# Rows of 32 experts carried by indirect DMA instead of one-hot matmuls, with neighbouring experts interleaved

## What is computed

```
B, S, D = 2, 256, 256 (512 tokens);  E, G, K = 32, 8, 4;  hidden H = 512;  CAP_FACTOR = 1.25
scores of groups and experts -> the 4 best groups, in these the 4 best experts of each token
gate = softmax over the chosen experts
slot = how many earlier tokens chose the same expert; only slots below 80 = 512/32*4*1.25 are kept
out  = x + shared_expert(xn) + sum over kept choices of gate * expert_e(xn)
expert_e(v) = (silu(v @ wg[e]) * (v @ wu[e])) @ wd[e]          # 256 -> 512 -> 256, f32
```

## Time and profile before

| what | us |
|---|---|
| three runs | 2159.97, 2161.23, 2163.57; median 2161.23 |
| the profiled execution | 2161.95, with a span of 2160.1 from first to last instruction |
| PE busy | 1865.0 (86% of the span) |
| DVE, ACT, POOL busy | 1178.5, 865.4, 178.5 |
| mean granted PE clock | 0.918 of full speed |
| router block (first load issued to the last product of the shared expert) | 1031.7 to 1069.4 |
| experts (first pass of up to the sum with the residual) | 1072.65 to 1367.42 |

### The profile page before, as it was taken

The page is one execution under the profiler, slowest core; times in us unless marked ns, Lnnn a source line. Parts: engine busy times, 40 slices in busy tenths (PEclk is TensorE's granted clock), DMA queues, the critical chain, the costliest instruction groups (busy, mean ns, idle before and its releaser), DMA issues. The chain is left out here.

```text
span 2160.1 us, 38703 instructions
## 1 busy us (share of the span) xinstructions
PE 1865.0 (86%) x12958; PEld 1076.0 (50%) x12958; DVE 1178.5 (55%) x2155; ACT 865.4 (40%) x1654; POOL 178.5 (8%) x335
## 2 busy tenths in 40 slices
PE   8999799999999446588799999599999999383598
PEld 4444334444444224357599999344444444152476
DVE  5777588888886455364300000388887885372400
ACT  2222156666667123134211111166666666021121
POOL 2222200000000000010000000000000000000000
PEclk9999889999999768799799999699999999686699
DMA  5586654433340530000396665334343340502242
GB/s 187 185 223 192 161 86 62 59 58 58 58 58 16 135 42 1 0 1 17 114 262 225 226 196 171 48 45 60 58 58 58 58 62 12 82 8 80 78 136 68
DMA packets 148041, 200.20 MB, mean 93 GB/s; under 512 B 24712, under 2 KB 121744, under 8 KB 141608
## 3 DMA queue, kind: packets, MB, share of 16 engines
q1 hardware_dynamic: 145900, 197.34, 40.2%
q10 hardware_dynamic: 2064, 1.87, 0.3%
HBM read 160.25 MB, written 38.94 MB: 92 GB/s over the span
## 5 line engine op out<-in xcount | busy, mean ns | idle before, releaser
L1079 ACT ACTIVATE probs<-ps 128x512 f32<-128x512 f32 x1024 | 573.8, 596 | 287.7 <-PE ps L1006 276.3
L1091 DVE TENSOR_REDUCE top<-ps 128x1 f32<-128x1024 f32 x512 | 601.0, 1219 | 35.8 <-PE ps L987 33.4
L987 PE MATMUL ps<-kst,qst 105*128 105x512 bf16 x1024 | 318.7, 394 | 35.8 <-POOL qst L945 27.8
L1006 PE MATMUL ps<-qst,kst 105*128 105x256 bf16 x2048 | 344.6, 276 | 2.3 <-DVE qst L1103 1.8
L1020 PE MATMUL ps_o<-probs,vst 128*32 128x256 f32 x4096 | 328.6, 393 | 0.8 <-ACT probs L1079 0.8
L1006 PEld LDWEIGHTS ps<-qst,kst 105*128 105x128 bf16 x2048 | 176.3, 100 | 215.0 <-ACT probs L1079 66.1
L987 PEld LDWEIGHTS ps<-kst,qst 105*128 105x128 bf16 x1024 | 65.9, 98 | 189.8 <-DVE top L1091 90.5
L2035 DVE TENSOR_TENSOR hT<-silu,ps_h 128x320 f32<-128x320 f32 x32 | 15.6, 488 | 263.0 <-ACT silu L1996 263.0
L1020 PEld LDWEIGHTS ps_o<-probs,vst 128*32 128x32 f32 x4096 | 80.8, 108 | 109.9 <-issue 89.8
L477 PE MATMUL ps_k<-ctxT,wk 128*128 128x512 f32 x256 | 121.8, 599 | 2.1 <-DVE square_weights L642 2.1
L1959 PEld LDWEIGHTS ps_h<-xe,wgu 128*128 128x128 f32 x1024 | 119.3, 192 | 3.0 <-ACT xe L1985 0.2
(11 more groups left out here) (305 smaller groups left out, 2257.6 us busy)
## 6 DMA issues: line engine op xcount, KB each, us to landing
kst<-kd SPq DMA_DIRECT2D x384, 128.0 KB
kd<-kp SPq DMA_DIRECT2D x64, 384.0 KB, 2.6
wgu<-in_L_ffn_wg_dram SPq DMA_DIRECT2D x32, 512.0 KB, 3.8
wgu<-in_L_ffn_wu_dram SPq DMA_DIRECT2D x32, 512.0 KB, 4.6
wd<-in_L_ffn_wd_dram SPq DMA_DIRECT2D x32, 512.0 KB, 3.9
w<-in_L_ffn_w_dram SPq DMA_DIRECT2D x16, 1024.0 KB, 5.4
ctx_sb<-in_ctx_dram SPq DMA_DIRECT2D x16, 512.0 KB, 5.8
vd<-square_weights SPq DMA_DIRECT2D x16, 512.0 KB, 4.1
```

Of the source, the lines that this page charges most:

```text
L987: mm = pe.matmul(ps1[:, u % 2, x * 512:(x + 1) * 512], qst[:, m, qt * P:(qt + 1) * P], kst[:, m, c * W1 + x * 512:c * W1 + (x + 1) * 512], ...
L1006: mm = pe.matmul(ps2[:, u % 2, x, :], kst[:, m, kt * P:(kt + 1) * P], qst[:, m, :], start=True, stop=True)
L1079: nc.scalar.activation(probs[:, u % SLOTS, :, :], ps2[:, u % 2, :, :], ACT.Exp).then_inc(probs_ready, 1)
L1091: v.tensor_reduce(top[:, b, u // NC1, u % NC1:u % NC1 + 1], ps1[:, u % 2, :], AX, ALU.max).then_inc(mx, 1)
```

## The change

- route0 and the block of the experts become one block. There are no one-hot matrices any more: disp, comb, combT, gather, combine and the transposes of comb are gone, on PE, DVE, POOL and ACT.
- DVE makes, beside the gate, for each token the four row numbers (expert * 80 + slot) of its kept choices (row) and their shares (share). A choice that isn't kept gets a number out of bounds.
- A DRAM tensor expert_rows_in (2560 rows of 1 KB) is filled with zeros by SP, and then POOL scatters the rows of xn into it by 16 indirect DMAs (4 tiles x 4 choices, 128 rows each).
- For each expert SP loads its 80 rows (xr), PE turns them by two transposes (turn), ACT copies them to xe. After down, ACT copies ye, and SP stores it to expert_rows_out in DRAM.
- At the end POOL gathers the rows back by 16 indirect DMAs (back), and DVE adds them with 16 multiply-adds (128x256), after shared expert and residual have been put into dst earlier.
- PE's order for one expert is: turn(e+2), up(e+1), down(e). ps_h has two buffers (4 banks); ps_y lies in acc.
- SP's order for one expert is: rows of e+2 (xr), wgu of e+2, then, after ye of expert e is copied, wd of e+2, the store of ye.
- The loads for the next cross attention (kst, vall) are all issued ahead of the first xr; those of qall come in the following block (pieces_to_dram, before=), and qall is allocated only there.

The core of the diff (names that only move are left out):

```diff
-def route0(pr, st, xn, xT, acc, ahead):
+def experts0(pr, xn, xT, residual, dst, next_cross):
...
             @block.sync
...
-                ahead(sp)
+                sp.wait_ge(zero_set, 1)
+                sp.dma_start(xed.rearrange("(p r) d -> p r d", p=P), bc(zeros[:, :], 1, NROWS // P)).then_inc(zeroed, 16)
+                for e in range(2):
+                    load_gu(e)
+                    load_d(e)
+                for m in range(NBUF):
+                    next_cross.load_constant_rows(sp, m)
+                    next_cross.load_k(sp, m // B, m)
+                for part in range(VPARTS):
+                    next_cross.load_v(sp, part)
+                sp.wait_ge(scattered, 16 * NT * TOPK)
+                for e in range(2):
+                    load_x(e)
+                for e in range(E0):
+                    if e + 2 < E0:
+                        sp.wait_ge(x_turned, e + 1)
+                        load_x(e + 2)
+                        sp.wait_ge(h_made, e + 1)
+                        load_gu(e + 2)
+                    sp.wait_ge(y_copied, e + 1)
+                    if e + 2 < E0:
+                        load_d(e + 2)
+                    sp.dma_start(yed[e * CAP0:(e + 1) * CAP0, :], ye[:, e % 2, :]).then_inc(y_out[e % 2], 16)
+
+            @block.gpsimd
+            def _(pool):
+                nc.gpsimd.memset(zeros[:, :], 0.0).then_inc(zero_set, 1)
+                pool.wait_ge(zeroed, 16)
+                pool.wait_ge(row_ready, 1)
                 for t in range(NT):
+                    for k in range(TOPK):
+                        nc.gpsimd.indirect_dma_start(
+                            xed, bass.IndirectOffsetOnAxis(row[:, t, k:k + 1], 0), xn[:, t, :], None,
+                            bounds_check=NROWS - 1, oob_is_err=False).then_inc(scattered, 16)
+                pool.wait_ge(sh_added, 1)
+                nc.gpsimd.memset(back[:, :, :, :], 0.0).then_inc(zero_set, 1)
+                pool.wait_ge(zero_set, 2)
+                for b in range(2):
+                    pool.wait_ge(y_out[b], 16 * E0 // 2)
+                for t in range(NT):
+                    for k in range(TOPK):
+                        nc.gpsimd.indirect_dma_start(
+                            back[:, t, k, :], None, yed, bass.IndirectOffsetOnAxis(row[:, t, k:k + 1], 0),
+                            bounds_check=NROWS - 1, oob_is_err=False).then_inc(came_back[t], 16)
...
+                def turn(e, b, first=False):
+                    pe.wait_ge(x_in[b], 8 * (e - b) + 16)
+                    if not first:
+                        pe.wait_ge(x_copied, e - 1)
+                    for c in range(C):
+                        mm = pe.transpose(xview[:, b, c, :], xr[:, b, c * P:(c + 1) * P], pr.cf("ident")[0:CAP0, 0:CAP0])
+                    mm.then_inc(x_turned, 1)
...
                 def expert(e, b, place):
...
+                    if not place.startswith("last"):
+                        turn(e + 2, b)
+                    if place != "last":
+                        up(e + 1, 1 - b, first=(place == "first"))
+                    down(e, b, first=(place in ("first", "second")))
+
+                turn(0, 0, True)
+                turn(1, 1, True)
+                up(0, 0, True)
+                experts(pe, expert)
...
+                for k in range(TOPK):
+                    link(v.tensor_tensor(a[:, :, :], dest[:, :, :], bc(dtop[:, :, k], 2, E0), ALU.is_equal))
+                    link(v.tensor_tensor(a[:, :, :], a[:, :, :], gate[:, :, :], ALU.mult))
+                    link(v.tensor_reduce(share[:, :, k], a[:, :, :], AX, ALU.add))
...
                 experts(dve, expert)
+                for t in range(NT):
+                    dve.wait_ge(came_back[t], 16 * TOPK)
+                for k in range(TOPK):
+                    for t in range(NT):
+                        last = v.scalar_tensor_tensor(out=dst[:, t, :], in0=back[:, t, k, :], scalar=share[:, t, k:k + 1],
+                                                      in1=dst[:, t, :], op0=ALU.mult, op1=ALU.add)
+                    link(last)
```

More of the change, by code:

```diff
@@ L750, in split3_negated, with pieces_to_dram @@
     link(v.tensor_tensor(pieces[2], scratch, pieces[1], ALU.subtract))
-def pieces_to_dram(pr, xT, jobs, values=None):
+def pieces_to_dram(pr, xT, jobs, values=None, before=lambda sp: None):
     nc = pr.nc
@@ L809, in _ @@
             def _(sp):
+                before(sp)
                 def load_back(j):
@@ L1741, in route0, with experts @@
+        came_back = [pr.sem(st, f"came_back{t}") for t in range(NT)]
+        def experts(eng, body):
+            body(0, 0, "first")
+            body(1, 1, "second")
+            with eng.Fori(1, E0 // 2 - 1) as i:
+                for b in range(2):
+                    body(2 * i + b, b, "")
+            body(E0 - 2, 0, "last but one")
+            body(E0 - 1, 1, "last")
         with nc.Block() as block:
@@ new lines, in up @@
+                def up(e, b, first=False):
+                    pe.wait_ge(x_copied, e + 1)
+                    pe.wait_ge(gu_in[b], 16 * (e - b) + 32)
+                    if not first:
+                        pe.wait_ge(h_done, e - 1)
+                    for i in range(2):
+                        for f in range(FT0):
+                            for c in range(C):
+                                mm = pe.matmul(hview[:, b, i, f, :], wgu[:, b, i, c, f * P:(f + 1) * P], xe[:, b, c, :],
+                                               start=(c == 0), stop=(c == C - 1))
+                    mm.then_inc(h_made, 1)
@@ new lines, in down @@
+                def down(e, b, first=False):
+                    pe.wait_ge(h_done, e + 1)
+                    pe.wait_ge(d_in[b], 8 * (e - b) + 16)
+                    if first:
+                        pe.wait_ge(base_ready, 1)
+                    else:
+                        pe.wait_ge(y_copied, e - 1)
+                    for f in range(FT0):
+                        mm = pe.matmul(ps_y[0:CAP0, b, :], hT[:, b, f, :], wd[:, b, f, :],
+                                       start=(f == 0), stop=(f == FT0 - 1))
+                    mm.then_inc(y_made, 1)
```

322 lines of the change are left out of this document (121 added, 201 removed).

## The result

| | median | lowest to highest |
|---|---|---|
| before | 2162.03 us (4 runs) | 2159.97 to 2163.57 |
| after | 2403.74 us (4 runs) | 2400.33 to 2404.54 |

The ratio is 1.1116, with a 95% interval of 1.1096 to 1.1135: the changed kernel is slower by 241.7 us, where +266 was forecast (2427, range 2300 to 2490). The profiled execution has a span of 2401.2 us in place of 2160.1.

A forecast was written before the change was run, and what follows sets the result against it. The prediction took PE's own instructions to bound the kernel (busy 293.54 of 294 us). First up at 1112, experts 490 and tail 31 gave 1633 in place of 1367.4, +266, so 2427 us, range 2300 to 2490.

The forecast's parts named there:

- PE's own work: In the expert loop: up, turn and down take 5.48 us an expert, 175 for 32, a gain of 119 us alone.
- The pause: Before turn, PE waits 5.0 us for rows queued behind wd and the store, 29 times, 145 us.
- Its lower bound: The wait before turn if the rows need not wait for wd: 3.8 us in place of 5.0.
- The clock, 0.50 in the bursts: In the experts: the clock stays at 0.50, bursts last 10.8 us, and experts with pauses take 490 us.
- a rise inside down: The clock rising during an expert's down would save up to 0.8 us each, 26 in all.
- A clock that returns inside each burst: Rival for the experts: the clock rises within every burst, period 12.9 us, total 2334 or 2305; chance 0.20.
- A clock that holds: Rival for the experts: the full clock lasts through the pauses, period 10.5 us, total 2257; chance 0.08.
- Rows in time: Rival at turn: rows land without a wait, 5.48 us a turn, total 2112, faster than before; chance 0.05.
- The head: Ahead of the experts: SP's queue delays the first rows, so up starts at about 1112, 39 us later.
- The tail: Behind the last down: store, 16 gathers at 1.1 us, landing and additions take 31 us, where 3.7 were.
- The sum: The block's end: 1112 + 490 + 31 = 1633 in place of 1367.4, so +266 us.

The follow-up runs named there:

- e2: The changed kernel with SP issuing the loads of rows and wgu as soon as their buffers are free; 2112.29 us, ratio 0.9771.
- e4: The changed kernel with the rows' load issued first behind the copy of ye, ahead of wd and the store; 2313.34 us, ratio 1.0705.
- e3: The changed kernel with 11 unread matmuls of 256 columns ahead of turn in each of the 28 middle turns; 2275.23 us, ratio 1.0528.
- e7: e2 with the 16 loads of vall moved behind the last store of ye; 2103.13 us, ratio 0.9744.
- e1: The changed kernel with SP issuing the load of an expert's rows one expert earlier; 2185.33 us, ratio 1.0112.
- e8: e7 with 42 unread matmuls ahead of the first turn and DVE's additions done tile by tile; 2093.41 us, ratio 0.9696.
- e5: e4 with 76 unread matmuls of 256 columns in PE's idle time ahead of the first turn; 2306.62 us, ratio 1.0685.

## Why the prediction was right, step by step

**PE's own work, 5.48 us for an expert at the full clock.** Right: 5.54 and 5.44 from turn to turn in e2. The 119 us that this saves are real, and e2 collects most of them: 185 us from first up to the end of the last down in place of 291, with two ups and a down at the low clock in it.

**The pause, 5.0 us, 29 times.** Right: 5.24, 29 times. The forecast read SP's order and put the rows behind wd and the store. Their load is issued 1.46 us behind down, as forecast, and the landing behind wd was sized well, too. Its lower bound, 3.8 us with nothing to queue for, was 0.4 too high, as an 80 KB load lands in 1.9 us (e4) and not in the 2.8 less 0.5 that I took from 256 KB. That e4's wait is shorter still, 2.4, is its earlier issue, 0.43 behind down. For wd, store and rows in a line the Trainium skill (DMA: Bandwidth & Descriptors, "Anatomy of one DMA") would have given 4.2 by its 2.0 us and 436 GB/s, which are fitted there on DMAs that GpSimd issues, while these are SP's. The trace has 5.24, and wd alone takes 4.0 where the page's terms make 3.2.

**The clock, 0.50 in the bursts.** Right in the main, and the term with the largest error in it. Forecast were bursts of 10.8 us; (477 - 152) / 32 = 10.2 were measured, 20 us less in all. The forecast named this as a lower bound, a rise inside down worth up to 26 us, and that is where most of it happens: down takes 2.51 us at 1303.96 and 3.49 at 1319.02, by whether the rise comes inside it. 13 downs are shortened by it, 12 us together. Some 5 us more are the last expert, whose up has no pause ahead of it and takes 3.69 us at the full clock, which the forecast left out. The earlier trace rows had shown that a pause of 5 us takes the clock down, that it can stay low through a stretch of narrow passes, and both held in the new loop.

**The rivals.** A clock that returns inside each burst wanted a period of 12.9 us, the forecast 15.8; from turn(3) to turn(31) it is 15.6 ((1562.97 - 1125.69) / 28). A clock that holds wanted 10.5. It is what e3 shows, at 10.97 from up to up ((1443.49 - 1103.73) / 31, the first turns at the low clock), but only with the pauses filled. Rows in time gave 2112 for a wait that is hidden, with first up at 1112, 175 us for the experts and 31 for the tail. e2 is that case, built by another order on SP: 2112.29, with 1105.7, 185 and 31.6. That the totals agree to 1 us is luck: the experts took 10 us more than 175 and the head 6 less than 1112, and the trace with these terms is of an execution of 2118.38. To be faster than before, the wait would have to fall to 1.7 us at the full clock; even e4's 2.4 doesn't get there.

**The head, first up at 1112.** The mechanism was right (e7: it is the queue), the size 9 us too high: 1102.68. SP's issues in the head of the changed kernel:

```profile
1034.70 0.58 SPq L1806 DMA_DIRECT2D expert_rows_in<-zeros  x1
1035.32 7.42 SPq L1789 DMA_DIRECT2D wgu<-in_L_ffn_wg_dram  x1
...
1061.71 32.21 SPq L336 DMA_DIRECT2D vall<-vd  x16
1093.96 8.67 SPq L1797 DMA_DIRECT2D xr<-expert_rows_in  x3
```

Bytes and order are as the forecast had them; the rates are not. The DMA view of 1034 to 1104 gives them in 40 slices of 1.75 us:

```profile
GB/s 51 309 273 385 386 388 387 399 406 371 384 368 260 206 201 211 206 225 211 225 218 207 312 388 382 339 348 382 350 358 353 323 344 349 351 348 315 159 17 47
```

Zeros and weights ran at 368 to 406 GB/s from 1039 to 1055, where the forecast had 329 for them, the keys then at 201 to 225 where it had 159, and the values behind them mostly at 339 to 388. Both rates that I took from the earlier trace rows were low here. The stretch of 260 to 280, read as keys alone, has only the last few loads of keys in it, and behind them weights and rows of weights in loads of 128 and 256 KB. And 329, a mean over 20 us with the starts and ends of loads in it, is below the 380 to 420 that most of the full slices of the same 20 us reach.

**The tail, 31 us.** 31.6 was measured, by terms that don't all agree. In the changed kernel, from the last copy of ye on:

```profile
1579.70 0.37 ACT L1969 COPY ye<-acc 80x256 f32<-80x256 f32 x1 [1.36 <-PE acc L1914]
1582.61 1.05 POOL L1846 DMA_INDIRECT back<-expert_rows_out,row  x1 [493.31 <-DMA expert_rows_out<-ye]
...
1602.22 1.00 POOL L1846 DMA_INDIRECT back<-expert_rows_out,row  x1 [0.30 <-issue]
1604.43 6.80 DVE L2055 SCALAR_TENSOR_TENSOR other_x<-back,share,other_x 128x256 f32<-128x256 f32 x16 [27.23 <-DMA back<-expert_rows_out,row]
```

A gather follows the one before after 1.30 us (1.00 busy and 0.30 between), where 1.1 was taken, the middle of 0.4 and 1.8. 15 of these intervals are 19.6 us. The additions took 6.8, as forecast (6.6). Copy, issue and landing of the store took 2.9 and not 3.4, and the last landing 2.2 behind its issue and not 2.8. Too little for the gathers (2.0) and too much for the landings (1.1) cancelled in part, and the forecast's own terms add up to 30.4, rounded up to 31: the hit to 1 us is partly luck.

**The sum.** Head 9 too high and experts 13 too high (pauses 7 too low, bursts 20 too high), tail right to 1 us: 22 us, and with that 1633 - 22 = 1611, where the block does end. Of the 24 us by which +266 was too high, these two terms are 22; the others lie outside the block. Pauses and bursts missed in opposite directions, so the 13 are smaller than the larger of their errors.

## What stays open

In e1 there are 18 waits of 2.0 us on average, between turn and up or inside up, and the clock is higher than with e4's 29 pauses of 2.4 us. From 1275 to 1340 it even holds 1.00 through waits of up to 2.42 us in most turns, while in e8 it falls 3.0 us after the end of the fill, with PE idle for only 1.4 of them. How soon it falls in a pause differs as well: 0.7 us after PE stopped at 1366.2 in the kernel before, 2.1 and 3.2 us after in the two pauses of the changed kernel shown above. So the length of a pause alone does not decide. Whether it is the pauses' place, or that 14 experts of e1 have none, no kernel here separates. Why the last gather lands 3.7 us later beside the values (e7) was not separated either. The gathers and SP's loads are on different queues (q0 and q1 on the page of the profile), so what they share is the 16 DMA engines and the memory.

## What to carry to other kernels

Before a load is moved in a queue, ask when its request is *issued*, and what stands ahead of it on that queue. Here the change had made PE's work 40% smaller, and a request that waited for the copy of the previous result made it 11% slower; the same instructions with the loads issued when their buffers come free are 2.3% faster than before. A pause on TensorE can cost twice when it comes in every turn: once as idle time (here 152 us), once as the half clock that follows it (here at least 128). Read the granted clock of the bursts before counting on either, since e1 held the full clock through waits that e4 did not. And a large load that nobody needs soon (here the values) belongs behind the small one for which the engine waits, with an eye on what it then runs beside.

## What was not expected of the hardware

- An 80 KB load lands 1.9 us after its issue in an empty queue and 3.7 behind 512 KB and 80 KB on the same one.
- The granted clock rises when a burst is nearly over and stays up for 2 to 3 us of the idle time behind it, 1.00 from 1307.0 to 1308.5 with PE at rest since 1306.5, and to 1325.5 with PE at rest since 1322.5.
- Pauses of 2.4 us in turns of 12 already keep the bursts mostly at the low level (e4), whether PE came to them at the full clock or not (e5). Waits of up to 2.4 us between turn and up left it at 1.00 in e1 from 1275 on.
- An indirect DMA of 128 rows of 1 KB occupies POOL for 1.0 us, with 0.30 to the next, to DRAM and from it alike (0.97 and 0.30 for the scatter).
- An issue can hold SP itself for long when much stands ahead on its queue: the one behind the zero-fill of 2.6 MB took 7.42 us, and the 16 of the values 32.21 together, where such an issue takes 0.5 in the loop. That the queue was full is the likely reason, and not shown.
